# Context statistics sent through DRAM to all partitions, and the normalised context formed transposed on GpSimd

## The reference

```python
def block0(x, ctx):                              # 16 heads of 16
    x1 = layernorm(x + mha(x, x, causal=True))   # attention 0
    x2 = layernorm(x1 + mha(x1, ctx * live))     # attention 1
    return layernorm(x2 + relu(x2 @ fc1 + b1) @ fc2 + b2)
def block1(x, ctx):                              # attention 2: 16 heads of 64, 4 key heads
    h, kv = rmsnorm(x) * w, rmsnorm(ctx) * w
    x = x + softmax(rope(h @ Wq) @ rope(kv @ Wk).T / 8 + mask) @ (kv @ Wv) @ Wo
    n = rmsnorm(x) * w2
    return x + (silu(n @ Wgate) * (n @ Wup)) @ Wdown
def block2(x, ctx):                              # attention 3
    q, c = layernorm(x), layernorm(ctx)
    return x + softmax(heads(q @ Wq + bq) @ heads(c @ Wk + bk).T / 4) @ (c @ Wv + bv) @ Wo + bo
def block3(x, ctx, mask):                        # attention 4
    s = 0.5 * (s0 * mask) + 0.5 * s0             # s0 = scores of x with the plain ctx
    return layernorm(x + softmax(clip(s, -50, 50)) @ v @ Wo + bo)
```

## Time and profile before

| what | value |
|---|---|
| time, median of 3 runs | 4020.08 us (4019.24 to 4020.08) |
| profiled execution | 4024.71 us |
| its span, first to last instruction | 4022.9 us |
| TensorE busy, share of the span | 98% |
| VectorE, ScalarE, GpSimd | 73%, 66%, 31% |
| mean granted TensorE clock | 0.986 of full speed |

### The profile page before, as it was taken

One profiled execution on the slowest core, in us unless ns is written; L12 is line 12 of the kernel. 1 busy time (PEld: TensorE's weight loads), 2 busy tenths in 40 slices (PEclk: granted clock), 3 DMA queues, 4 the chain that ended last, 5 costly groups with the idle time before them and its releaser, 6 DMA issues.

```text
span 4022.9 us, 115273 instructions
## 1 busy us (share of the span) xinstructions
PE 3927.7 (98%) x44448; PEld 3431.3 (85%) x44448; DVE 2945.7 (73%) x10721; ACT 2672.9 (66%) x8449; POOL 1227.7 (31%) x2247
## 2 busy tenths in 40 slices
PE   6999999999999999999999999999999999999997
PEld 5788888888888888888888888888888888888885
DVE  3677777777777777777777777777777777777763
ACT  2666766766766767667667667667667667667663
POOL 1232332332333333332332332322323323323331
PEclk6999999999999999999999999999999999999997
DMA  3000000000000000000000000000000000000000
GB/s 145 2 18 18 10 18 18 10 17 15 12 18 10 18 18 10 18 18 10 18 18 10 17 17 10 18 17 10 18 17 10 18 17 10 18 12 15 18 3 5
DMA packets 66495, 69.61 MB, mean 17 GB/s; under 512 B 7456, under 2 KB 64800, under 8 KB 65056
## 3 DMA queue, kind: packets, MB, share of 16 engines
q1 hardware_dynamic: 65952, 62.25, 4.9%
HBM read 53.83 MB, written 8.39 MB: 15 GB/s over the span
## 4 chain that ended last, share of the span: by engine, by line
PE 89%; DVE 6%; ACT 2%; issue 2%; POOL 1%; DMA 0%; SPq 0%; DVEq 0%; POOLq 0%; ACTq 0%
PE gen_ps L467 54%; PE gen_ps L459 16%; PE gen_ps L589 6%; PE scores_ps L563 5%; PE gen_ps L601 3%; PE scores_ps L549 3%; PE scores_ps L556 2%; PE scores_ps L542 1%; ACT oT L699 1%; DVE wide L887 1%; DVE zn L932 1%; DVE v L992 1%; DVE rdenm L929 1%; DVE plainT L995 1%; DVE res L996 1%
## 5 line engine op out<-in xcount | busy, mean ns | idle before, releaser
L467 PE MATMUL gen_ps<-actT,w_sb 128*128 128x128 f32 x10752 | 1352.7, 279 | 14.1 <-DMA w_sb<-weights_dram 9.3
L467 PEld LDWEIGHTS gen_ps<-actT,w_sb 128*128 128x128 f32 x10752 | 1267.5, 193 | 70.2 <-issue 48.1
L699 ACT ACTIVATE probT<-gen_ps 128x512 f32<-128x512 f32 x1024 | 576.3, 633 | 218.1 <-PE gen_ps L459 214.8
L788 POOL TENSOR_TENSOR rstd<-ve,consts 128x1 f32<-128x1 f32 x448 | 282.7, 631 | 1436.5 <-DVE ve L939 850.9
L733 ACT ACTIVATE prob<-scores_ps,negmax 128x128 f32<-128x128 f32 x2048 | 566.6, 415 | 200.5 <-DVE negmax L977 200.4
L459 PE MATMUL gen_ps<-consts,prob 128*128 128x128 f32 x4096 | 605.6, 279 | 17.4 <-ACT prob L733 7.2
L459 PEld LDWEIGHTS gen_ps<-consts,prob 128*128 128x128 f32 x4096 | 473.0, 142 | 130.2 <-ACT prob L733 59.2
L467 PE MATMUL gen_ps<-w_sb,actT 128*128 128x256 f32 x1792 | 466.6, 383 | 2.9 <-ACT actT L699 2.1
L467 PE MATMUL gen_ps<-w_sb,wide 128*128 128x256 f32 x2056 | 466.7, 380 | 1.3 <-DVE wide L1117 1.0
L849 POOL TENSOR_SCALAR prob<-prob,rden 128x128 f32<-128x128 f32 x1024 | 362.1, 373 | 320.7 <-DVE rden L1050 320.7
L699 ACT ACTIVATE actT<-gen_ps 128x256 f32<-128x256 f32 (+1 forms) x512 | 238.5, 466 | 292.9 <-PE gen_ps L459 292.9
(11 more groups left out here) (116 smaller groups left out, 6013.4 us busy)
## 6 DMA issues: line engine op xcount, KB each, us to landing
actT<-xT_dram SPq DMA_DIRECT2D x64, 128.0 KB, 2.2
ctx_rms<-x_dram SPq DMA_DIRECT2D x64, 128.0 KB, 2.2
ctx<-ctx_dram SPq DMA_DIRECT2D x64, 128.0 KB, 2.2
ctxT<-ctxT_dram SPq DMA_DIRECT2D x64, 128.0 KB, 2.3
mask<-mask_dram SPq DMA_DIRECT2D x128, 64.0 KB, 2.1
out_dram<-res SPq DMA_DIRECT2D x64, 128.0 KB, 1.7
w_sb<-weights_dram SPq DMA_DIRECT2D x2, 2048.0 KB, 18.7
w_sb<-weights_dram SPq DMA_DIRECT2D x2, 1024.0 KB, 20.3
```

What stands on the lines that cost most here:

```text
L467: last = nc.tensor.matmul(ps, lhsT(c), rhs(c), start=(c == 0), stop=(c == chunks - 1))
L699: release(nc.scalar.activation(dst, take(act, name, b)[:, 0:width], ACT.Copy), name, b)
L788: nc.gpsimd.tensor_tensor(dst, src, const("expo")[:, 0:width], ALU.pow)\
```

## The change

Statistics take another way, and the context is no longer transposed for attentions 2 and 3:

- `ctx_norms` on GpSimd makes the two reciprocal roots and a third number per row, minus mean times root. SyncE writes the three numbers of 128 rows to DRAM (`stat_dram`), waits, and reads them back to every partition: `stat_bc`, 3 x 128 numbers along the free axis.
- A new GpSimd event `ctx_rms` multiplies `ctxT` with the RMS row into `ctx_nT`, the same tile as before under another view. `ctx_ln`, once `kv2` has read that, writes `ctxT` times root, and then adds the shift in a second operation.
- `tr` 2 and `tr` 3 transpose two blocks in place of four; ScalarE copies 256 wide in place of 512. `kv2` and `keys` 3 read `ctx_nT`.
- SyncE's queue has, per element, the wait for `cshift` of the element before, the write, the wait for it, and the read, between the loads of b and the next wait for `out_ready`.
- `LIFE`, `ONCE` and `PERIOD` are new, and `BANK_LATE` names `m0` in place of two turns. The Bacc object gets a `dynamic_dma_scratch_size` of 8192.

The core of the diff:

```diff
-PERIOD = 69.731652
+PERIOD = 81.171106
...
-    ("ctx_ln", 2, 0, {"POOL": 137.062}),
+    ("ctx_rms", 2, 0, {"POOL": 190.846}),
+    ("ctx_ln", 2, 0, {"POOL": 211.759}),
...
-BANK_LATE = {"t32", "t33"}
+BANK_LATE = {"m0"}
...
+                elif a == 3:
+                    pe.wait_ge(sem("ctx_ln"), b + 1)
...
-                src = ctxT[:, g, :, :] if a == 4 else actT[:, g, 2:4, :]
+                src = ctxT[:, g, :, :] if a == 4 else ctx_nT[:, g, :, :] if a == 3 else actT[:, g, 2:4, :]
...
-                    pe.wait_ge(sem("ctx_rms"), b + 1)
-                    transposes("tr2", b, halves(zn[:, g, :]) + halves(ctx_rms[:, g, :]))
+                    transposes("tr2", b, halves(zn[:, g, :]))
...
-                    pe.wait_ge(sem("ctx_ln"), b + 1)
-                    transposes("tr3", b, halves(zn[:, g, :]) + halves(ctx_ln[:, g, :]))
+                    transposes("tr3", b, halves(zn[:, g, :]))
...
-                    read_out(pe, "tr2", b)
+                    pe.wait_ge(sem("ctx_rms"), b + 1)
                     ps = begin("kv2", b)
...
-                    width = D if a == 4 else 2 * D
+                    width = 2 * D if a == 1 else D
...
-                    rsqrt(cve[:, g, :], crstd[:, g, :], "cve", "crstd", b, 2)
+                    rsqrt(cve[:, g, :], crstd[:, g, 0:2], "cve", "crstd", b, 2)
                     pool.wait_ge(sem("crstd"), b + 1)
-                    nc.gpsimd.tensor_scalar(ctx_rms[:, g, :], ctx[:, g, :], crstd[:, g, 1:2], 0.0,
-                                            ALU.mult, ALU.add).then_inc(sem("ctx_rms"), 1)
+                    nc.gpsimd.tensor_scalar(crstd[:, g, 2:3], cmv[:, g, 0:1], crstd[:, g, 0:1], -1.0,
+                                            ALU.mult, ALU.mult).then_inc(sem("cshift"), 1)
+                elif name == "ctx_rms":
+                    pool.wait_ge(sem(f"stat_in{g}"), 16 * (b // G + 1))
+                    pool.wait_ge(sem("res_0"), b + 1)
+                    once(pool, ctxT_sem(b), 16 * (b // G + 1))
+                    nc.gpsimd.tensor_tensor(ctx_nT[:, g, :, :], ctxT[:, g, :, :],
+                                            stat_bc[:, g, 1, :].unsqueeze(1).to_broadcast([P, C, S]), ALU.mult)\
+                        .then_inc(sem("ctx_rms"), 1)
                 elif name == "ctx_ln":
-                    j, use = plan["tr2", b]
+                    j, use = plan["kv2", b]
                     once(pool, bank_full[j], use)
-                    nc.gpsimd.tensor_scalar(ctx_ln[:, g, :], ctx[:, g, :], cmv[:, g, 0:1], crstd[:, g, 0:1],
-                                            ALU.subtract, ALU.mult).then_inc(sem("ctx_ln"), 1)
+                    nc.gpsimd.tensor_tensor(ctx_nT[:, g, :, :], ctxT[:, g, :, :],
+                                            stat_bc[:, g, 0, :].unsqueeze(1).to_broadcast([P, C, S]), ALU.mult)\
+                        .then_inc(sem("ctx_scaled"), 1)
+                    pool.wait_ge(sem("ctx_scaled"), b + 1)
+                    nc.gpsimd.tensor_tensor(ctx_nT[:, g, :, :], ctx_nT[:, g, :, :],
+                                            stat_bc[:, g, 2, :].unsqueeze(1).to_broadcast([P, C, S]), ALU.add)\
+                        .then_inc(sem("ctx_ln"), 1)
...
+                def spread_stats(b):
+
+                    sp.wait_ge(sem("cshift"), b + 1)
+                    with nc.allow_non_contiguous_dma(reason="three numbers a row"):
+                        sp.dma_start(stat_d[b].rearrange("k s -> s k"), crstd[:, b % G, :])\
+                            .then_inc(sem(f"stat_out{b % G}"), 16)
+                    sp.wait_ge(sem(f"stat_out{b % G}"), 16 * (b // G + 1))
+                    sp.dma_start(stat_bc[:, b % G, :, :].rearrange("p k s -> p (k s)"),
+                                 stat_d[b].rearrange("k s -> (k s)").partition_broadcast(P))\
+                        .then_inc(sem(f"stat_in{b % G}"), 16)
...
+                spread_stats(0)
...
+                    if b <= B:
+                        spread_stats(b - 1)
```

235 lines of the change are left out of this document (119 added, 116 removed).

## The result

| | before | after |
|---|---|---|
| median | 4019.7 us (4014.1 to 4020.1, 4 runs) | 4091.9 us (4081.8 to 4095.5, 4 runs) |
| span of the profiled execution | 4022.9 | 4089.6 |
| usual period | 60.85 | 61.45, and 35 longer ones |

The changed kernel is slower: ratio 1.0177, 95% interval 1.0164 to 1.019. The forecast was 3986 with a range up to 4030, so direction and size were both wrong.

What follows compares the result with a forecast made beforehand. TensorE's queue was taken as the bound. Removed transposes (28 us) plus moves (6 us) gave 34 us off the profiled 4024.7, so 3990.7, and a 3986 us median; likeliest 3970 to 4005, range 3945 to 4030.

Steps and rivals of the forecast that it cites:

- What bounds the kernel: TensorE, 98% busy, sets the 60.86 us period; only less work or less waiting in its queue shortens it.
- Removed transposes: Four fewer transposes in `tr` 2 and `tr` 3 take 0.45 us per element off TensorE's queue: 28 us gained.
- Turn of the period: From the scores of attention 3 to `queries` 1, reordered: 12.25 us instead of 12.69, gain 0.4 us per period.
- Behind `down`: `zT` 4 waits about 0.4 to 0.5 for VectorE, `tr` 3 0.1 to 0.2: loss 0.3 us per period.
- GpSimd's operations: Context normalisation adds 1.0 to 1.2 us per element on GpSimd, 31% busy: no cost unless it meets VectorE.
- SyncE's transfers: Two small statistics transfers per element fit in 23 us: nothing, with 0 to 2 us for the first elements.
- Fill and drain: Time before and after the even stretch, together, stays within 8 us of 378.5.
- Slower: GpSimd at the turn: Rival: `tr` 1 waits for GpSimd's chain, late by one more VectorE rotation, 1.2 us per period: 4058; chance 0.12.
- Waiting takes the gain: Rival: one element's chain sets the period, about 4015, or GpSimd contention stretches VectorE, 4021; chance 0.17.
- the late statistics: Rival: transfers take over 23 us and TensorE waits at `kv2`; at 25 us, 4106; chance 0.03.
- the table saves more: Rival: turn waits vanish altogether, 3938, or the 274 ns transpose reading holds, 3950; chance 0.16.
- Net of all moves: -0.1 us per period: All reordering together, between -0.6 and +0.5 us per period: -6 us over 59.9 periods.

Runs made afterwards that it cites:

- before_notr: Kernel before without the four transposes of the normalised context (keys 3 and `kv2` read the query side): 4015.5 us, ratio 0.9994.
- before_notrp: Kernel before without the four context transposes and with GpSimd's two operations behind the sum of `down` swapped: 3989.4 us, ratio 0.9927.
- before_foldp: Kernel before, transposes kept, `rdenm` folded into VectorE's normalisation reading PSUM, GpSimd's two operations behind the sum of `down` swapped: 4006.4 us, ratio 0.997.
- before_newtable: Kernel before, all its operations and no transfers, in the order of the new table with the new late banks: 4086.7 us, ratio 1.017.
- after_nodma: Changed kernel without the two statistics transfers, the broadcast statistics filled with ones once: 4057.1 us, ratio 1.0087 to the kernel before.
- after_fold: Changed kernel with `rdenm` folded into VectorE's following normalisation that reads PSUM: 4021.3 us, ratio 0.9999 to the kernel before.
- mix: No context transposes, statistics written as 12-byte rows, `rdenm` folded, in the order of the kernel before: 4003.9 us, ratio 0.9965 to the kernel before.
- mixp: As mix, with GpSimd's bias add put ahead of the root of the variance behind the sum of `down`: 3979.2 us, ratio 0.9898.
- mixr: As mix, with `tr` 3 behind the first `q2` half and the second half behind it, ahead of queries 3: 4061.3 us, ratio 1.0108.

## Why the prediction was wrong, step by step

**What bounds the kernel.** TensorE's queue does, and starts were the right thing to read. But "a period gets shorter only by less work in TensorE's queue or by less waiting in it" was then used one-sidedly: the waits that show were listed, and the ones that would appear once their cover goes were looked for only at the places that moved.

**Removed transposes, 28 us.** A step whose reason was wrong. "In the even stretch they are [on the path]" was taken for granted; in the old order their removal gives 3 us (before_notr). The size was nearly right: with `zn` of `tr` 3 on time 29 us come through (before_notrp), of which 3 to 6 are the swap's own by before_foldp, which leaves 23 to 26 for the transposes, an estimate. The rows to see it were in the trace: `zn` of L1127 ends 0.08 us before `tr` 3 starts. In the new order the four transposes and the exchange of GpSimd's operations are worth 30 us (before_newtable to after_nodma; 33 by the ratios), which is the 28 of the sum. So in the kernel after this term did come, because the new order puts `tr` 3 ahead of `tr` 2: luck, as the prediction took it from the old order, where it fails. The measured 4092 is therefore not due to this term but to the next ones and the transfers.

**Turn of the period, gain 0.4.** The step that failed with the largest price. Predicted 12.25 us from `values` 0 to `queries` 1, measured 13.42 where 12.69 was the old value: a loss of 0.73. The list of TensorE's work was right. What failed is a sentence: "at its new places VectorE mostly reads PSUM". One operation there, `rdenm`, reads and writes SBUF, is tiny, and stands exactly beside the q2 pair. Everything behind it on VectorE (`zn`, the live flag, `kv2`) moves by 1.0 us, and TensorE waits for two of them. I had counted the bank wait at 0.3; it is 0.71. Without `rdenm` (after_fold) the stretch takes 12.67, the old value, so the 0.4 was not there either; two waits of 0.2 each are left, for the masked context at `tr` 1 and for the copy ahead of `queries` 1. The prediction did name the right sign of being wrong, "VectorE's SBUF operations longer than before".
The contention was seen, with the right pair, but priced by GpSimd's added time, at most 35 us, as a rival of chance below 0.17. Its price doesn't follow GpSimd's added time but what meets what: 47 us by the usual period (after_fold), of which the same fold wins 8 before. The rule in the Trainium skill, "GPSIMD Engine Reference", "Key points" (GpSimd shares its SBUF interfaces with VectorE, contention in VectorE's 2-port modes or with two SBUF inputs) agrees with `rdenm` at 1.24 beside GpSimd and 0.24 alone, and it counted for more than the prediction let it. Which of the two cases of the rule it is, no run here shows.

**Behind `down`, loss 0.3.** Measured: scores 4 to `values` 0 take 27.94 us against 29.74 - 1.75 (q2 half) - 0.45 (transposes) = 27.54 for the same work in the old kernel, 0.4. Right in sign and near in size; the wait at `zT` 4 is 0.58, that at `tr` 3 0.22.

**GpSimd's operations, +1.0 to +1.2 us.** Four operations of 724, 726, 731 and 267 ns against 479 and 1215: +0.75. "Cost nothing, unless it meets VectorE" was not tested by itself. One new meeting shows: VectorE's L962 takes 0.87 us beside `ctx_rms` (L817) in each element, 0.72 beside `ctx_ln` (L814) before and 0.48 alone.

**SyncE's transfers, nothing.** Half right. That the two fit was right: the write took 9.0 us and the read 5.0, 14 of the 23 us, and `ctx_rms` is never late (in the even stretch it starts some 12 us after the read has landed; "some 15" was the forecast). The failed part is the place where the price was looked for: only at who waits for the data. Engines that do not wait for the write stop while it is under way, 35 us in all. The Trainium skill's rule ("DMA: Bandwidth & Descriptors", "Rules for kernel authors": a strided last dimension becomes one descriptor per element) was read right, and the trace agrees: packets under 512 bytes went from 7456 to 34080, 26624 more, of which 64 x 384 = 24576 are the write's. It was dismissed too soon, by the slack.

**Fill and drain.** "Within 8 us" held by the prediction's own bounds: what lies outside the 60 inner periods is 371.9 us before and 367.6 after. Ahead of the first `out2` and behind the last the spans shrank by 3.5 and 5.9. The 5.9 are not the change's: after_nodma, with the same order, has 74.3 us behind the last `out2`, as before (75.2), and after has 69.3 with a granted clock of 0.93 in the second 25 us of it, against 0.72 there and 0.68 before.

**Rivals.** "Slower: GpSimd at the turn", 4058, had place and size nearly: after_nodma takes 4057.1. But its mechanism, one more rotation of VectorE ahead of GpSimd, isn't what happened; there a VectorE operation waits for GpSimd. "Waiting takes the gain" is what before_notr shows in the old order, behind `down`, not by the chain of an element. No rival had two of these together, nor a transfer that costs without being waited for; so 4092 lay beyond everything but the late statistics. (In "the table saves more", the 274 ns reading gives 3986 - 42 = 3944 by the sum's own terms, not 3950.)

**The account.** The order +68 (before_newtable), the transposes and GpSimd's operations in that order -30 (after_nodma), the transfers +35: 4019.7 + 73 = 4092.7, measured 4091.9. The three are differences along one row of kernels from before to after, so their sum has to close. What the runs add is where each sits: the order at the turn and behind `down`, the transfers in the longer periods.

In short, two terms of the sum failed. "Net of all moves: -0.1 us per period" was +1.13 (0.73 at the turn, most of it `rdenm` waiting out GpSimd's q2 operation, and 0.4 to 0.5 behind `down`), 68 us in place of -6. "Nothing" for SyncE's transfers was 35 us.

## What to carry to other kernels

Before work is counted as gained, look at what ends last right behind it: if an operand of the next instruction becomes ready only as that instruction starts, the work was cover and its removal wins nothing until the operand comes earlier. Lay GpSimd's operations where VectorE reads PSUM or waits, and fold small SBUF-to-SBUF steps of VectorE into one that reads PSUM: a swap of two operations of GpSimd won 25 us here (mix to mixp). The same look is due before work is moved: a q2 half moved away uncovered another copy and cost 57 us (mix to mixr). Write small statistics in the longest contiguous runs there are, even if the reader must stride.
